# Graph message passing on one core: the edge stage on pairs of chunks, with a new order of GpSimd's work

## The chip, the cores and the metric

The kernel runs on one core of a Trainium2 chip. The metric is the device time of one execution in microseconds (us), the median over runs. The engines are TensorE (PE, its weight loads PEld), VectorE (DVE), ScalarE (ACT), GpSimd (POOL) and SyncE (SP, which only issues transfers). Each works through its own instructions in order and waits on semaphores.

## The reference

There are 50000 nodes with 256 numbers each and 12500 edges, sorted by destination. Two layers are computed; the change concerns the edges of the first.

```python
h = relu(layernorm(x))                      # every node
xn = layernorm(h) * ln_g + ln_b
q, k, v = xn @ Wq.T + bq, xn @ Wk.T + bk, xn @ Wv.T + bv
dk = silu(edge_attr @ Wdk.T + bdk);  dv = silu(edge_attr @ Wdv.T + bdv)
attn = silu(sum(q[dst] * k[src] * dk, 1)) * cosine_cutoff(edge_weight)
agg = segment_sum(v[src] * dv * attn[:, None], dst)
x = x + h + agg @ Wo.T + bo                 # end of layer 1
# layer 2: deg by src, dinv = rsqrt(deg), normalised gather over the edges (rows dst into src),
# then h @ (W, W1), relu, @ W2, added to x
```

## The kernel before, in words

The edges are cut into 98 chunks of 128 edges, one edge a partition; the nodes into 98 groups of 512 rows. Five stages follow each other: a set-up (weights transposed, degrees summed with one-hot matmuls, their inverse roots written to a table in DRAM), the edge stage of layer 1 (`messages`), the edge stage of layer 2 (`messages2`, 49 pairs of chunks), the node stage (`nodes`, 98 groups), and the last stores. `sums0` and `sums1` in DRAM hold the sums; they are filled with their first values by 512 KB transfers from SP (`rows_b`, `rows_0`), and for part of `sums0` from ACT in the first steps of the edge stage.

Each engine has its own function `messages(s)`, called once a step by `run_steps`; in it blocks for different chunks stand in a fixed order, `s.back(n)` being the chunk n steps back. For one chunk the edge stage does this:

- POOL gathers 128 rows of x for the destinations and 128 for the sources by indirect transfers (`gather_x`, four chunks ahead of use, into X2, a ring of four), and one number an edge from the table (`tab_d`).
- DVE takes the statistics of the two tiles (`bn_stats`, `bn_aggr`, L751 and L773) and adds eps (`ve`); POOL raises them to the power -0.5 (`inv_sqrt`, L476); DVE makes the bias `nb`. ACT computes the normalised relu into H2 (`m_h`). DVE takes the statistics of H2, in the same instructions as those of a later chunk; the same power call serves both; ACT scales H2 into Z2 (`m_z`).
- PE transposes Z2 and the edge attributes (bank 0 and 7), ACT copies bank 0 to `zT`, DVE copies the attributes to `aT`. PE makes the 512 numbers dk, dv (bank 1; ACT takes the silu into `DS`), k and v (banks 2 and 3), q (bank 4), each with a bias from a matmul on three rows (`ones3`, `bias3`).
- DVE: k * dk (`KD`), the sum with q (`at`), ACT its silu (`sa`), DVE times the cutoff (`aa`) and the message `MSG`. DVE also compares the destinations within the chunk (`EQ`) and finds which edge is the first of its node (`cnt`, `fst`, `sidx`); the others are sent to dump rows.
- PE sums equal destinations (MSG with EQ, bank 5), DVE copies it (`ST`), PE multiplies with Wo (bank 6), ACT copies it (`UB`), POOL adds its rows to `sums0` by an indirect transfer (`scatter_add`, L480).
- DVE keeps x + h of the destinations (`kept`) and ew * dinv (`norm`) for `messages2`.

POOL's order in a step before is: the two row gathers of chunk s, the power for chunk s-1, the table gather of s-1, the scatter of chunk s-11. Every scatter waits for the one before to have landed (`m_sc`).

Of the kernel before, what the change touches and what calls it, by code (L numbers as in the profile page):

```python
# [5 lines left out]
P = 128  # L6
D = 256
R = 64
N = 50000
# [4 lines left out]
G = 4  # L14
# [6 lines left out]
MESSAGE_STEPS = 11  # L21
# [5 lines left out]
FILLS_STEP = 4  # L27
# [62 lines left out]
def build(nc, x, src, dst, edge_attr, edge_weight, ln_g, ln_b, Wq, bq, Wk, bk, Wv, bv, Wo, bo,  # L90
          Wdk, bdk, Wdv, bdv, W, b, W1, b1, W2, b2, out):
    ctx = ExitStack()
    with ctx:
# [13 lines left out]
        sums0 = nc.dram_tensor("sums0_dram", (ROWS, D), F32).ap()  # L107
# [12 lines left out]
        ones3 = sb("ones3", [3, P], BF16)  # L120
        leave3 = sb("leave3", [3, 2])
# [9 lines left out]
        def place(taken, shape, dt=F32):  # L131
# [4 lines left out]
            at0 = taken[0]  # L136
# [11 lines left out]
        def temp(shape, dt=F32):  # L148
# [18 lines left out]
        rows3 = temp([3, 4 * D])  # L167
        part3 = temp([3, 4 * D])
        piece = temp([3, 4 * D], BF16)
        bias3 = sb("bias3", [3, 4 * D], BF16)  # L170
# [25 lines left out]
        dump_f = sb("dump_f", [P, 1])  # L196
        dump_i = sb("dump_i", [P, 1], I32)
# [32 lines left out]
        X2 = [CG[1][:, i, :].rearrange("p (a d) -> p a d", a=2) for i in range(4)]  # L230
        H2 = [CG[2][:, i, :].rearrange("p (a d) -> p a d", a=2) for i in range(4)]
        Z2 = ring("z2_", 2, [P, 2, D])
        ib = ring("ib_", 2, [P, 2, 3], I32)
        attr = ring("attr_", 4, [P, R])
        row_d = ring("row_d_", 4, [P, P], I32)

        st = ring("st_", 2, [P, 4, 6])
        mv = ring("mv_", 2, [P, 4, 2])
        ve = ring("ve_", 2, [P, 4, 1])
        rs = ring("rs_", 2, [P, 4, 1])  # L240
        nb = ring("nb_", 2, [P, 4, 1])
        zT = ring("zT_", 2, [P, 2 * KC, P])
        aT = ring("aT_", 2, [R + 1, P])
        DS = ring("ds_", 2, [P, 2 * D])
        KD = ring("kd_", 2, [P, D])
        junk = sb("junk", [P, D])
        junk_e = sb("junk_e", [P, P])
        at = ring("at_", 2, [P, 1])
        sa = ring("sa_", 2, [P, 1])
        aa = ring("aa_", 2, [P, 1])  # L250
        EQ = ring("eq_", 2, [P, P])
        MSG = ring("msg_", 2, [P, D])
        ST = ring("stt_", 2, [P, KC, P])
        UB4 = sb("ub4", [P, 4, D])
        UB = [UB4[:, i, :] for i in range(4)]
        tab_d = ring("tab_d_", 2, [P, 2, 1])
        cnt = ring("cnt_", 2, [P, 2])
        fst = ring("fst_", 2, [P, 2])
        sidx = ring("sidx_", 2, [P, 2], I32)
        m_ib, m_row, m_attr = sem("m_ib"), sems("m_row", 4), sems("m_attr", 4)  # L260
        m_x, m_tab = sems("m_x", 4), sems("m_tab", 2)
        (m_st, m_mv, m_ve, m_rs, m_nb, m_h, m_z, m_xh, m_T, m_zT, m_aT, m_D, m_qkv, m_ds, m_kd, m_at, m_sa, m_aa,
         m_eq, m_cnt, m_fst, m_idx, m_msg, m_S, m_ST, m_U, m_UB, m_keep) = [
            sem("m_" + n) for n in ("st mv ve rs nb h z xh T zT aT D qkv ds kd at sa aa eq cnt fst idx msg S ST U "
                                    "UB keep").split()]
# [9 lines left out]
        EQ2 = [halved(CG[2], i)[:, 2:4, :] for i in range(2)]  # L275
        EN = ring("en_", 2, [P, 2, 2 * P])
# [61 lines left out]
        def _(sp):  # L338
# [21 lines left out]
            for i, v in enumerate((bq, bk, bv, b2)):  # L360
                sp.dma_start(rows3[:, i * D:(i + 1) * D],
                             v.rearrange("(a d) -> a d", a=1).broadcast_to([3, D])).then_inc(s_ldw, 16)
# [7 lines left out]
            for i in range(FILLS_FIRST):  # L370
                sp.dma_start(group(sums0, Step(i)), rows_b).then_inc(s_fill, 16)

# [4 lines left out]
            LATER = 8  # L377

            def load_edges(s):
                k = s  # L380
                if k.within(EC):
                    n = k.off if k.reg is None else None
                    rows = ET if n == EC - 1 else P
                    if k.past(4):

                        pass_on(sp, (m_T, k.value(-3)))
                    sp.dma_start(attr[k.slot(4)][0:rows, :],
                                 edge_attr[bass.ds(k.value(0, P), rows), :]).then_inc(m_attr[k.slot(4)], 16)
                    if k.past(4):

                        pass_on(sp, (m_eq, k.value(-3)))
                    sp.dma_start(row_d[k.slot(4)][:, 0:rows],
                                 dst[bass.ds(k.value(0, P), rows)].rearrange("(a e) -> a e", a=1)
                                 .broadcast_to([P, rows])).then_inc(m_row[k.slot(4)], 16)

                k = s.back(LATER)
                if k.within(EC):

                    sp.dma_start(group(sums1, k), rows_0).then_inc(s_fill1, 16)

            assert NG == EC
            run_steps(sp, EC, LATER, 4, 4, load_edges)
# [47 lines left out]
        def _(pool):  # L450
# [36 lines left out]
            def gather_x(k):  # L487

                for i in range(2):
                    gather(X2[k.slot(4)][:, i, :], x, ib[k.pair()][:, k.slot(2), i:i + 1], last_node, m_x[k.slot(4)])  # L490


            pool.wait_ge(m_ib, 2)
            for i in range(4):
                gather_x(Step(i))

            def messages(s):
                k = s
                if k.within(EC) and k.past(4):

                    w = [(m_xh, k.value(-3))]
                    if k.slot(2) == 0:
                        w.append((m_ib, k.turns(2, 1)))
# [836 lines left out]
```

## Time and profile before

| | us |
|---|---|
| median of 3 runs (lowest, highest) | 2039.34 (2038.46, 2040.52) |
| the profiled execution, its own time | 2035.36 |
| its span in the trace | 2033.7 |
| mean granted TensorE clock, share of full | 0.900 |
| busy: PE, DVE, ACT, POOL | 1667.5, 1406.6, 1193.9, 1389.7 |

The busy times are sums over all stages; what matters for the change is the stretch from about 107 us, where the DVE begins with chunk 0, to about 848 us, where the first gather of `messages2` starts. In rows of the timeline the first number is the start and the second the duration, in us from the start of the span.

### The profile page before, as it was taken

To read this page: it belongs to the slowest core of one execution; us is meant where nothing else is said; L and a number is where in the kernel's file an instruction comes from. 1 tells how busy PE (TensorE), PEld (TensorE's weight loads), DVE (VectorE), ACT (ScalarE), POOL (GpSimd) and SP (SyncE) were. 2 spreads that over 40 slices of the span, in tenths; PEclk is the share of its full clock that TensorE was granted. 3 is DMA by queue.
4 is the path that set the end of the run, shared out by engine and by line. 5 is a ranking of instruction groups with operands and counts; after the bars stand their busy time and mean duration, and the time that the engine had idled before them with its cause. 6 is when DMAs were issued, how large, how long until landed. Compare 5 with 4: busy or idle time off the path is not lost.

```text
span 2033.7 us, 32020 instructions
## 1 busy us (share of the span) xinstructions
PE 1667.5 (82%) x6331; PEld 1026.7 (50%) x6331; DVE 1406.6 (69%) x5976; ACT 1193.9 (59%) x2320; POOL 1389.7 (68%) x1047
## 2 busy tenths in 40 slices
PE   4939999999999999344444541999999999999999
PEld 2315454445544545233333331676767666666666
DVE  7956666666666666355545547888888888888883
ACT  5925555554555454122222124998898989898884
POOL 2047888888888885488888877666666666666660
PEclk9959999999999999666656655999999999999999
DMA  7996555555555556244445458899999999999991
GB/s 247 418 363 204 142 146 150 140 143 143 154 140 142 145 144 203 47 87 89 89 89 90 87 102 206 234 272 273 263 272 269 269 270 268 272 269 267 266 256 72
DMA packets 170410, 391.76 MB, mean 193 GB/s; under 512 B 38847, under 2 KB 85872, under 8 KB 170368
## 3 DMA queue, kind: packets, MB, share of 16 engines
q1 hardware_dynamic: 105920, 257.96, 37.6%
q0 software_dynamic: 59552, 115.52, 31.0%
q10 hardware_dynamic: 4896, 17.83, 2.2%
q8 instruction: 13, 0.21, 0.0%
q14 instruction: 29, 0.24, 0.0%
HBM read 211.37 MB, written 179.85 MB: 192 GB/s over the span
## 4 chain that ended last, share of the span: by engine, by line
POOL 31%; DMA 22%; PE 18%; issue 16%; DVE 9%; SPq 2%; ACT 1%; POOLq 1%; DVEq 0%; ACTq 0%
POOL sums_dram L480 8%; DMA sums_dram<-ub,sidx 8%; POOL cg L484 7%; DMA out_dram<-cg 6%; POOL kept L567 6%; PE bank L1312 6%; PE bank L1301 6%; POOL b_rs L476 4%; DMA cg<-in_x_dram,ib 4%; PE bank L1169 3%; DVE cg L929 3%; POOL tab_d L484 3%; DMA cg<-sums_dram,ic 3%; POOL rs L476 2%; PE bank L1291 1%
## 5 line engine op out<-in xcount | busy, mean ns | idle before, releaser
L480 POOL DMA_INDIRECT sums_dram<-ub,sidx x196 | 318.9, 1627 | 96.8 <-issue 42.7
L1301 PE MATMUL bank<-kept,w 128*128 128x512 f32 x784 | 354.6, 595 | 0.0
L1312 PE MATMUL bank<-w_sb,kept 128*128 128x256 f32 x1568 | 354.3, 379 | 0.0
L567 POOL TENSOR_TENSOR kept<-kept 128x1024 f32<-128x1024 f32 x98 | 233.4, 2382 | 176.4 <-DVE cg L929 176.4
L1267 PE MATMUL bank<-cg,en 128*128 128x256 f32 x392 | 178.3, 634 | 204.4 <-ACT cg L1074 197.6
L1312 PEld LDWEIGHTS bank<-w_sb,kept 128*128 128x128 f32 x1568 | 297.9, 190 | 81.9 <-issue 46.4
L484 POOL DMA_INDIRECT cg<-in_x_dram,ib x196 | 206.3, 1052 | 78.9 <-issue 58.4
L1267 PEld LDWEIGHTS bank<-cg,en 128*128 128x128 f32 x392 | 120.5, 322 | 262.1 <-issue 236.4
L476 POOL TENSOR_TENSOR b_rs<-b_ve,minus_half 128x8 f32<-128x8 f32 x102 | 209.8, 2057 | 23.7 <-DVE b_ve L946 23.7
L476 POOL TENSOR_TENSOR rs<-ve,minus_half 128x4 f32<-128x4 f32 (+1 forms) x149 | 145.2, 974 | 101.4 <-DVE ve L781 91.6
L1301 PEld LDWEIGHTS bank<-kept,w 128*128 128x128 f32 x784 | 142.2, 191 | 141.9 <-issue 141.8
L1095 ACT ACTIVATE kept<-kept,b_nb,b_rs 128x256 f32<-128x256 f32 x392 | 202.2, 589 | 13.4 <-DVE b_nb L919 13.4
L1105 ACT ACTIVATE kept<-kept,b_nb,b_rs 128x256 f32<-128x256 f32 x392 | 202.3, 589 | 9.6 <-DVE b_nb L919 9.6
L1224 PE MATMUL bank<-qkv_w,zT 128*128 128x512 f32 x392 | 198.0, 628 | 0.0
L1065 ACT ACTIVATE ub<-bank 128x512 f32<-128x512 f32 x49 | 29.2, 597 | 273.6 <-DMA sums_dram<-ub,sidx 273.6
L1014 ACT ACTIVATE ub<-bank 128x256 f32<-128x256 f32 x98 | 37.7, 384 | 258.0 <-PE bank L1251 243.0
L751 DVE BATCH_NORM_STATS2 st<-cg 128x6 f32<-128x256 f32 x196 | 73.7, 418 | 163.4 <-DMA cg<-in_x_dram,ib 158.8
L957 DVE SCALAR_TENSOR_TENSOR kept<-cg,dinv,kept 128x256 f32<-128x256 f32 x392 | 163.9, 480 | 5.0 <-issue 2.2
L1086 ACT ACTIVATE kept<-bank 128x1024 f32<-128x1024 f32 x98 | 100.4, 1024 | 85.7 <-PE bank L1291 85.7
L929 DVE TENSOR_TENSOR cg<-kept,bank 128x1024 f32<-128x1024 f32 x98 | 119.6, 1220 | 39.3 <-PE bank L1312 34.7
L1291 PE MATMUL bank<-identity,kept 128*128 128x128 f32 x784 | 103.9, 276 | 51.6 <-DVE kept L957 51.5
L934 DVE BATCH_NORM_STATS2 b_st<-kept 128x6 f32<-128x256 f32 x392 | 137.0, 412 | 3.2 <-DMA kept<-in_x_dram 3.2
(183 smaller groups left out, 3227.7 us busy)
## 6 DMA issues: line engine op xcount, KB each, us to landing
sums_dram<-cg SPq DMA_DIRECT2D x162, 512.0 KB
kept<-in_x_dram SPq DMA_DIRECT2D x97, 512.0 KB, 5.8
kept<-sums_dram POOLq DMA_DIRECT2D x97, 512.0 KB, 9.9
cg<-sums_dram SPq DMA_DIRECT2D x97, 512.0 KB, 8.8
out_dram<-cg SPq DMA_DIRECT2D x97, 512.0 KB, 9.7
sums_dram<-cg ACTq DMA_DIRECT2D x34, 512.0 KB
row_d<-in_dst_dram SPq DMA_DIRECT2D x97, 64.0 KB
row_s<-in_src_dram SPq DMA_DIRECT2D x48, 128.0 KB
```

Of the source, the lines that this page charges most:

```text
L476: pool.tensor_tensor(to, var, minus_half[:, 0:width].rearrange("p (a b) -> p a b", b=1), ALU.pow).then_inc(done, 1)
L480: pool.indirect_dma_start(sums, bass.IndirectOffsetOnAxis(idx, 0), rows, None, bounds_check=last_row, compute_op=ALU.add).then_inc(done, 16)
L484: pool.indirect_dma_start(to, None, table, bass.IndirectOffsetOnAxis(idx, 0), bounds_check=bound, oob_is_err=True).then_inc(done, 16)
L567: pool.tensor_tensor(X1[k.slot(8)], X[k.slot(4)], H[k.slot(2)], ALU.add).then_inc(g_xh, 1)
L929: dve.tensor_tensor(OUT[k.slot(2)], X1[k.slot(8)], bank[:, to:to + 2, :].rearrange("p a b -> p (a b)"), ALU.add).then_inc(g_fin, 1)
L957: ins = dve.scalar_tensor_tensor(AG[k.slot(2)][:, at0], S1[k.slot(4)][:, at0], dinv[:, bass.ds(k.value(0, G) + j, 1)], H1[k.slot(2)][:, at ...
L1095: ins = act.activation(H1[k.slot(2)][:, j * D:(j + 1) * D], X1[k.slot(8)][:, j * D:(j + 1) * D], ACT.Relu, bias=b_nb[k.back(-4).slot(2)][: ...
L1105: ins = act.activation(H[k.slot(2)][:, j * D:(j + 1) * D], X[k.slot(4)][:, j * D:(j + 1) * D], ACT.Relu, bias=b_nb[k.slot(2)][:, j, :], sc ...
L1224: pe.matmul(bank[:, 2 + q, :], zT[q][:, KC + c, :], qkv_w[:, c, D:3 * D], start=False, stop=(c == KC - 1))
L1267: ins = pe.matmul(bank[:, q, to * D:(to + 1) * D], EN[q][:, i, to * P:(to + 1) * P], H1e[q][:, i, :], start=(i == 0), stop=(i == 1))
L1301: ins = pe.matmul(bank[:, 2 + m, :], w01[:, c, m * P:(m + 1) * P], hT[k.slot(2)][:, c * GN:(c + 1) * GN], start=(c == 0), stop=(c == KC - 1))
L1312: ins = pe.matmul(to, rT[k.slot(2)][:, c * GN + j * P:c * GN + (j + 1) * P], w2_sb[:, c, :], start=False, stop=(c == KC - 1), skip_group_c ...
```

## The change

All engines' `messages(s)` now handle a pair of chunks in a step: 49 pairs (`EP`), with 7 steps of depth instead of 11.

- POOL is unrolled in full. In its step p it does: the two scatters of pair p-7; the power for pair p-2 (one call on 128x6: the roots for both normalisations, the second variance being worked out as var(h) + eps times the first); `gather_x(p)`, that is four row gathers, the destinations' straight into `kept`; the two table gathers of pair p-1.
- DVE's step s works for the pairs a = s-1 (first statistics), g = s-2 (second statistics), z = s-3 (bias `nbz`, `kept`) and m = s-4 (attention, message), interleaved in the order of the diff.
- ACT's relu now runs before the first root is known (it only subtracts the mean, into G2), and ACT copies `ST`.
- The bias is folded into the weights: element 0 of each tile Z2 is a constant 1, since the normalised row sums to zero; the six bias matmuls of a pair go. The edge attributes arrive transposed by the host, so that their transpose and the copy to `aT` go too.
- EQ of the second chunk in a pair spans 256 edges (both chunks), so that equal destinations within a pair are summed once, and the two scatters of a pair may be in flight together: PE has 6 matmuls of 128 columns a pair for that instead of 4.
- SP fills `sums1` by two transfers a pair; ACT fills the rest of `sums0` by 8 transfers a step (4 before). `norm` is one instruction after the stage. The temporaries of the set-up lie at the other end of `kept`.

```diff
-            def messages(s):
-                k = s
-                if k.within(EC) and k.past(4):
-                    w = [(m_xh, k.value(-3))]
...
-                    gather_x(k)
-                k = s.back(1)
-                if k.within(EC + 2):
-                    inv_sqrt(ve[k.slot(2)][:, :, :], rs[k.slot(2)][:, :, :], m_ve, m_rs, k)
-                if k.within(EC):
...
-                    gather(tab_d[k.pair()][:, k.slot(2), :], table, ...
-                k = s.back(11)
-                if k.within(EC):
...
-                    scatter_add(sums0, sidx[k.pair()][:, k.slot(2):k.slot(2) + 1], UB[k.slot(4)], m_sc)
+            def gather_x(p):
+                if p >= 2:
+                    pool.wait_ge(m_h, p - 1)
+                for k in (2 * p, 2 * p + 1):
+                    gather(XS[k % 4], x, look[:, k, 1:2], last_node, m_x[p % 2])
+                    gather(kept[:, k, :], x, look[:, k, 0:1], last_node, m_x[p % 2])
+            def messages(p):
+                k = p - 7
+                if 0 <= k < EP:
+                    pool.wait_ge(m_UB, k + 1)
+                    pool.wait_ge(m_idx, k + 1)
+                    if k >= 1:
+                        pool.wait_ge(m_sc, 32 * k)
...
+                    for i in range(2):
+                        scatter_add(sums0, sidx[:, 2 * k + i:2 * k + i + 1], UB[2 * (k % 2) + i], m_sc)
+                k = p - 2
+                if 0 <= k < EP:
...
+                    pool.wait_ge(m_ve, k + 1)
+                    pool.tensor_tensor(RS[k % 2]..., VE[k % 2][:, 1:4, :, :]..., minus_half..., ALU.pow).then_inc(m_rs, 1)
+                if p < EP:
+                    gather_x(p)
+                k = p - 1
+                if 0 <= k < EP:
...
+                    for i in (2 * k, 2 * k + 1):
+                        gather(tab_d[:, i, :], table, look[:, i, 2:3], last_entry, m_tab)
```

```diff
+            def messages(s):
...
+                a, g, z, m = s.back(1), s.back(2), s.back(3), s.back(4)
+                if a.within(EP):
+                    q = a.slot(2)
+                    dve.wait_ge(m_x[q], a.turns(2, 64))
+                    for i in range(2):
+                        dve.bn_stats(st1[q][:, 0, i, :], XS[2 * q + i])
...
+                if z.within(EP):
+                    q = z.slot(2)
+                    dve.wait_ge(m_rs, z.value(1))
...
+                    dve.scalar_tensor_tensor(nbz[q][:, :, :], mv2[q][:, :, :, 0], -1.0, RS[q][:, 1:3, :, 0],
+                                             ALU.mult, ALU.mult).then_inc(m_nb, 1)
...
+                if g.within(EP):
+                    q = g.slot(2)
+                    dve.wait_ge(m_mv2, g.value(1))
+                    dve.wait_ge(m_ve1, g.value(1))
+                    dve.scalar_tensor_tensor(VE[q][:, 2:4, :, 0], VE[q][:, 0:2, :, 0], EPS, mv2[q][:, :, :, 1],
+                                             ALU.mult, ALU.add).then_inc(m_ve, 1)
```

The order of a step s after the change, in full (each with the waits that the prediction speaks of):

- DVE: a: 4 `bn_stats` of the gathered rows (waits `m_x`, both chunks' four gathers). m: `key(0)` (KD; waits `m_kv`, `m_ds`). z: `nbz` (waits `m_rs`, gives `m_nb`). a: 4 `bn_aggr`. m: `attend(0)`. a: `nm1` (gives `m_nm1`), eps. z: 2 `kept` (gives `m_keep`). m: 2 `EQ`. g: 4 `bn_stats` (waits `m_h`). m: 2 `cnt`, `key(1)` (waits `m_kv` and `m_ds` of the second chunk). g: 4 `bn_aggr`. m: `attend(1)` (waits `m_q`, gives `m_at`), `fst`. g: the last part of `VE` (gives `m_ve`). m: `sidx`, `aa` (waits `m_sa`), 2 `MSG` (gives `m_msg`).
- ACT: the fills (steps 2 to 6); m: `zT` of the first chunk; s-7: `UB`; m: `DS` of the first chunk; z: 2 of `Z2`, first chunk (waits `m_nb`); m: `zT` of the second chunk; z: 2 of `Z2`, second chunk; pair s-1: 4 relu (waits `m_nm1`, and `m_keep` of pair s-3; gives `m_h`); m: `DS` of the second chunk (gives `m_ds`); s-5: `ST`; m: the silu of `at`.
- PE: m: dk/dv, k/v (waits `m_zT`, and `m_msg` of the pair before) and q of the first chunk, transposes of the second; s-5: MSG with EQ; m: dk/dv, k/v, q of the second chunk; s-6: Wo; s-3: transposes of the first chunk.

## Rows read from the trace of the kernel before

**Rows 1.** Stretches: busy PE, PEld, DVE, ACT, POOL, granted clock, DMA share, GB/s.

```profile
400.00:600.00 200.00, 185.90 (x719) 100.59 (x720) 134.58 (x666) 102.19 (x228) 167.58 (x144) 1.00 0.55 145
...
900.00:1100.00 200.00, 100.28 (x219) 67.43 (x217) 103.36 (x486) 42.46 (x81) 167.19 (x136) 0.62 0.50 89
```

**Rows 2.** Groups of GpSimd's instructions, 200 to 800 us: busy, mean; idle before, releaser.

```profile
L484 POOL DMA_INDIRECT cg<-in_x_dram,ib x166 | 175.0, 1054 | 50.8 <-issue 50.8
L480 POOL DMA_INDIRECT sums_dram<-ub,sidx x86 | 139.4, 1620 | 29.6 <-issue 25.6 <-ACT ub L1014 4.0
L476 POOL TENSOR_TENSOR rs<-ve,minus_half 128x4 f32<-128x4 f32 x86 | 94.2, 1095 | 4.7 <-DVE ve L781 2.1
L484 POOL DMA_INDIRECT tab_d<-table_dram,ib x84 | 90.5, 1077 | 16.0 <-issue 14.1 <-DVE sidx L813 1.0 <-DVE norm L817 0.4
```

**Rows 3.** Timeline of GpSimd in one step of the edge stage.

```profile
501.82 1.07 POOL L484 DMA_INDIRECT tab_d<-table_dram,ib  x1 [0.19 <-issue]
503.20 1.62 POOL L480 DMA_INDIRECT sums_dram<-ub,sidx  x1 [0.30 <-issue]
505.13 1.07 POOL L484 DMA_INDIRECT cg<-in_x_dram,ib  x1 [0.31 <-issue]
506.51 1.03 POOL L484 DMA_INDIRECT cg<-in_x_dram,ib  x1 [0.31 <-issue]
```

**Rows 4.** Groups by form, whole span: the power at two widths.

```profile
L476 POOL TENSOR_TENSOR b_rs<-b_ve,minus_half 128x8 f32<-128x8 f32 x102 | 209.8, 2057 | 23.7 <-DVE b_ve L946 23.7
...
L476 POOL TENSOR_TENSOR rs<-ve,minus_half 128x4 f32<-128x4 f32 x100 | 109.3, 1093 | 94.5 <-DVE ve L781 91.6
```

**Rows 5.** Timeline of VectorE, ScalarE and one PE group in the same step.

```profile
502.29 0.60 ACT L1021 ACTIVATE zT<-bank 128x512 f32<-128x512 f32 x1
...
502.79 1.08 ACT L1030 ACTIVATE z<-cg,nb,rs 128x256 f32<-128x256 f32 x2
...
503.36 1.98 PE L1224 MATMUL bank<-qkv_w,zT 128*128 128x512 f32 x4
503.77 1.08 ACT L1039 ACTIVATE cg<-cg,nb,rs 128x256 f32<-128x256 f32 x2
...
504.70 0.75 DVE L751 BATCH_NORM_STATS2 st<-cg 128x6 f32<-128x256 f32 x2 [2.52 <-DMA cg<-in_x_dram,ib]
...
505.37 0.41 DVE L755 CUSTOM_DVE_ANT_0 junk<-bank,kd 128x256 f32<-128x256 f32 x1
505.70 0.08 DVE L755 DVE_READ_ACCUMULATOR2_ANT at<- 128x1 f32 x1
...
505.93 0.58 ACT L1054 ACTIVATE ds<-bank 128x512 f32<-128x512 f32 x1
...
506.60 0.38 DVE L773 BATCH_NORM_AGGREGATE mv<-st 128x2 f32<-128x6 f32 x4
...
508.76 0.16 DVE L741 SCALAR_TENSOR_TENSOR nb<-mv,rs 128x4 f32<-128x4 f32 x1
...
508.83 0.42 DVE L747 TENSOR_TENSOR kd<-bank,ds 128x256 f32<-128x256 f32 x1
```

**Rows 6.** Timeline of PE in the first steps of the stage.

```profile
137.24 1.12 PE L1205 MATMUL bank<-identity,z 128*128 128x128 f32 x4 [5.75 <-ACT z L1030]
...
140.74 3.78 PE L1224 MATMUL bank<-qkv_w,zT 128*128 128x512 f32 x4
```

**Rows 7.** The chain of waits in order of time: start, duration of the piece.

```profile
351.92 3.75 DMA cg<-in_x_dram,ib
...
499.54 5.14 DMA cg<-in_x_dram,ib
...
982.54 2.88 DMA cg<-sums_dram,ic
```

**Rows 8.** Timeline of GpSimd at both ends of the stage.

```profile
117.83 1.09 POOL L484 DMA_INDIRECT tab_d<-table_dram,ib  x1 [8.30 <-DMA table_dram<-dinv]
...
848.17 1.10 POOL L484 DMA_INDIRECT cg<-sums_dram,ic  x1 [2.51 <-DMA sums_dram<-ub,sidx]
```

More of the change, by code:

```diff
@@ L26 @@
 FILLS_FIRST = 64
[L27 removed]
+FILLS_STEP = 8
 CUTOFF = 5.0
@@ L257, in build @@
         cnt = ring("cnt_", 2, [P, 2])
         fst = ring("fst_", 2, [P, 2])
[L259 to L265, printed above, removed]
+        sidx = sb("sidx", [P, EC], I32)
@@ L530, in _ @@
+            pool.wait_ge(m_ib, 1)
+            for p in range(EP + MESSAGE_STEPS):
+                messages(p)
             pool.wait_ge(m_sc, 16 * EC)
@@ new lines, in messages, with scaled @@
+                if s.back(4).within(EP):
+                    silu_d(0)
+                def scaled(i):
+                    k = s.back(3)
+                    q = k.slot(2)
+                    act.wait_ge(m_nb, k.value(1))
+                    if k.past(1):
+                        act.wait_ge(m_T, k.value(-1, 2) + i + 1)
+                    for e in range(2):
+                        ins = act.activation(Z2[i][:, e, 1:D], G2[2 * q + i][:, e, 1:D], ACT.Identity,
+                                             bias=nbz[q][:, e, i:i + 1], scale=RS[q][:, 1 + e, i, :])
+                    ins.then_inc(m_z, 1)
@@ L1033, in messages @@
-                k = s.back(2)
-                if k.within(EC):
-                    act.wait_ge(m_nb, k.value(1))
-                    if k.past(4):
-                        act.wait_ge(m_xh, k.value(-3))
-                    for i in range(2):
-                        ins = act.activation(H2[k.slot(4)][:, i, :], X2[k.slot(4)][:, i, :], ACT.Relu,
-                                             bias=nb[k.slot(2)][:, i, :], scale=rs[k.slot(2)][:, i, :])
-                    ins.then_inc(m_h, 1)
-                k = s.back(7)
@@ L1180, in _ @@
                                     start=(k == 0), stop=(k == KC - 1))
+            for i, w in enumerate((0, 512)):
+                wide = min(512, 3 * D - w)
+                ins = pe.matmul(bank[:, i, 0:wide], first_row[:, :], qkv_w[:, 0, w:w + wide], start=True, stop=True)
             ins.then_inc(s_pre_pe, 1)
@@ new lines, in messages @@
+                if m.within(EP):
+                    project(0)
+                    turn(m, 1)
+                if f.within(EP):
+                    q = f.slot(2)
+                    pe.wait_ge(m_msg, f.value(1, 2))
+                    pe.wait_ge(m_eq, f.value(1))
+                    if f.past(1):
+                        pe.wait_ge(m_ST, f.value(0))
+                    for c in range(KC):
+                        own, rest = MSG[0][:, c * P:(c + 1) * P], MSG[1][:, c * P:(c + 1) * P]
+                        pe.matmul(bank[:, 5, c * P:(c + 1) * P], own, EQ[0][q][:, :], start=True, stop=False)
+                        pe.matmul(bank[:, 5, c * P:(c + 1) * P], rest, EQ[1][q][:, 0:P], start=False, stop=True)
+                        ins = pe.matmul(bank[:, 5, (KC + c) * P:(KC + c + 1) * P], rest, EQ[1][q][:, P:2 * P],
+                                        start=True, stop=True)
+                    ins.then_inc(m_S, 1)
@@ L1234, in messages @@
-                k = s.back(8)
-                if k.within(EC):
-                    pe.wait_ge(m_msg, k.value(1))
-                    pe.wait_ge(m_eq, k.value(1))
-                    if k.past(1):
-                        pe.wait_ge(m_ST, k.value(0))
-                    for c in range(KC):
-                        ins = pe.matmul(bank[:, 5, c * P:(c + 1) * P], MSG[k.slot(2)][:, c * P:(c + 1) * P],
-                                        EQ[k.slot(2)][:, :], start=True, stop=True)
-                    ins.then_inc(m_S, 1)
```

535 lines of the change are left out of this document (287 added, 248 removed).

## The prediction

> **What bounds the kernel now.** I read the stretches first, for where the edge stage lies and which engine is fullest. In it PE is busy 185.9 of 200 us at full clock, and POOL 167.6 [rows 1]. The groups of GpSimd's instructions then show why POOL looks less full than it is. From 200 to 800 us it did 86 chunks, 6.98 us each. Its busy time is 175.0 + 139.4 + 94.2 + 90.5 = 499.1 us, and nearly all of its idle time is "issue" (50.8 + 25.6 + 14.1 = 90.5 us), only some 10 us are waits for somebody [rows 2]. The timeline shows this issue time in place: 0.30 to 0.31 us ahead of each indirect transfer, 0.19 us behind the power [rows 3]. So POOL sets the pace before, with PE close behind, and each chunk costs what POOL's five instructions cost. The latencies (a gather takes 3.8 to 5.1 us from its start to landing [rows 7]) are mostly covered, because the gathers run four chunks ahead of use.
>
> The question for the change is therefore double: what POOL's work of a pair costs, and whether the new order still keeps the latencies off the path.
>
> **POOL's own work for a pair.** Four row gathers, 1.05 us each, and two table gathers, 1.08 [rows 2]; two scatters, 1.62; 0.31 us of issue ahead of each [rows 3]. The power on 6 numbers is not in the trace: 4 cost 1.09 and 8 cost 2.06 [rows 4], so between these; I take 1.57, about the middle. Sum: two scatters 3.86, power 1.57, first row gather 0.19 + 1.05, three more 4.08, two table gathers 2.78: 13.5 us a pair, against 13.96 before. What the unrolling saves in registers I cost at nothing, as the 0.31 us belongs to the transfers. If POOL still set the pace, the change would bring 0.5 us a pair.
>
> **The loop that the new order closes.** In its step p POOL waits for `m_ve` of pair p-2, does the power, and only then gathers the rows of pair p. `m_ve` of pair p-2 comes near the end of DVE's step p (g = s-2). DVE's step p+1 begins with the wait for exactly the rows of pair p (a = s-1). Nothing runs ahead: behind the waiting power stand the gathers on POOL's queue; behind the waiting `bn_stats` stands all of DVE's step on DVE's, the end of which releases the next power. The period C of a step is at least the way round:
>
> 1. *From the rows' landing to* `nb`: four `bn_stats`, two take 0.67 us from start to the next one's start, so 1.33; `key(0)` in between, 0.33 to the next start; `nbz` 0.16: 1.8 us [rows 5].
> 2. *ACT from* `m_nb` *to the second* `DS`: two of `Z2`, `zT`, two of `Z2`, four relu, then `DS`. Two 256-wide activations take 0.98 us from start to the next start (502.79 to 503.77), `zT` 0.50, `DS` 0.58 to its end: 4 x 0.98 + 0.50 + 0.58 = 5.0 us [rows 5], and 0.05 for the signal. DVE's own work meanwhile (statistics of g, `kept`, EQ, counts: some 4 us) is hidden under this; without ACT's queue it would bind at about 7.0 us instead of the 8.2 below.
> 3. *DVE from* `m_ds` *to* `m_ve`: `key(1)` 0.42, four `bn_aggr` 0.3, `attend(1)` 0.41 + 0.08 [rows 5], two small ones 0.2: 1.4 us. So landing to `m_ve` is D = 8.2 us if PE's k/v and q of the second chunk are there in time. They start when the second `zT` is done (1.8 + 0.98 + 0.60 = 3.4 us) and end at 3.5 + 1.98 + half of that = 6.5, in time at full clock.
> 4. *POOL from* `m_ve` *to the start of the last gather*: signal 0.05, power 1.57, issue 0.19, three gathers at 1.36: 5.9 us.
> 5. *The landing* L of the last gather from its start: 3.75 and 5.14 us in the edge stage, 2.88 in `messages2`, where no 512 KB fills run beside it [rows 7]. The fills of a pair are released by EQ, some 4 us into DVE's step, and 1 MB of them should be through before the gathers start, so I take 3.2, and 2.8 to 5.1 as bounds.
>
> With full clock throughout: 8.2 + 5.9 + 3.2 = 17.3 us, against 13.96 before.
>
> **PE's clock.** PE is busy 6.5 us a chunk before [rows 1]; without the bias matmuls and with one more matmul of MSG a chunk about 5.9, so 11.8 of 17.3 us. Its idle time comes in one piece: k/v of the second chunk waits for `zT`, which stands behind the scaling, which waits for `nb`: 5 to 7 us idle, ahead of just the matmuls that step 3 needs. After 5.75 us of idleness PE ran the same transposes and k/v projection at half speed (3.78 us instead of 1.98, the level of 1.2 GHz instead of 2.4) [rows 5, 6], and in `messages2`, with shorter pauses, the granted clock averages 0.62 [rows 1]. From half speed the second q is there at 3.5 + 3.78 + 1.7 = 9.0 us, and `m_ve` at 9.0 + 0.5 + 0.2 = 9.7 to 9.8. That is D's upper end; I take 9.4, since PE, two thirds busy, will not be slow each time. C = 9.4 + 5.9 + 3.2 = 18.5 us.
>
> The Trainium skill (TensorE: Matmul & The Clock Gate, "HAM oscillation") warns against this shape, bursts of matmuls parted by a wait for data, and has each burst start at the low clock. By it D would be 9.8 and the time some 18 us longer; the rows of the first steps agree with it.
>
> Of the landing, the Trainium skill (DMA: Bandwidth & Descriptors, "Anatomy of one DMA") gives about 2.0 us fixed and the bytes over 436 GB/s, so an estimate of 2.3 us for these 128 KB; the rows are all above, perhaps as theirs is from the start of GpSimd's instruction. With 2.3 us C would be 17.6 and the time 40 us shorter.
>
> **The whole stage.** Before, the first gather of `messages2` starts at 848.2 us [rows 8]. After: the power of step 2 comes after the first table gathers, which wait for the table, at 117.8 + 2 x 1.39 = 120.6 us [rows 8]. Steps 3 and 4 lack the attention part but have 8 fills a step in ACT's queue; my estimate is 16 us each, so `m_ve` of step 4 at 152. Steps 5 to 49 gather rows: 45 x C. Steps 50 to 52 have no rows to wait for and run at PE's pace, 11.5 us each; then S, ST, Wo and UB, about 3.5, and the last two scatters 1.93 + 1.55 + 2.51 to their landing [rows 8]: 44 us. End: 152 + 45 C + 44 = 196 + 45 C, which is 1028.5 for C = 18.5, 180 us later than before. Break-even is C = 14.5.
>
> The rest is nothing or small. The set-up loses the three-row bias work and gains `weights()` (six DVE instructions), both hidden under the wait for the table, until 117.8. DVE loses `ST`, `aT`, half of the small instructions, and gains wider EQ; ACT gains `ST`: in the loop these count only as in the sum above. The waits of the scatters (for UB, for the scatters of the pair before) come 5 us and more ahead of the power and are met a step earlier; the scatters and table gathers (6.6 us) run while DVE works, under C - 5.9 - 1.4. If the loop went away, they would be POOL's bound of 13.5. SP's fills have 18 us a pair instead of 14 and are ready earlier. The stages behind are the same code: no change.
>
> Sum: the profiled execution took 2035.4 us, 4 below the median. 2035.4 + 180 = 2215, and as a median 2219 us.
>
> **The rivals.**
>
> *Short loop.* PE stays warm and the rows land as in `messages2`: C = 8.2 + 5.9 + 2.8 = 16.9, end at 956.5, 2148 us as a median. For it: fewer fills beside the gathers, PE two thirds busy. Against it: the idle piece lies just ahead of the projection that counts.
>
> *Long loop.* The projections always start slow and the fills hold the gathers up: 9.8 + 5.9 + 5.1 = 20.8, 2323 us. PE's whole pair at half speed, 11.8 x 1.9 = 22, would be the pace itself; but PE busy without pause came back to full clock (3.78 us at 140.7, 1.98 at 503.4 [rows 5, 6]), so it shouldn't last.
>
> *POOL remains the bound, faster.* C = 13.5: end at 803.5, 1995 us. This needs D + L below 13.5 - 5.9 = 7.6 us, or rows that are gathered a step earlier than I read. Against it: ACT's and DVE's sum of 8.2 alone is above that, and so is DVE's own 7.0 with any landing of the rows. If half the loop were hidden by something I don't see, C would be near 14.5 and the time unchanged.
>
> **How the numbers follow.** Forecast (C 17.5 to 19.5, 2175 to 2264 us) 0.55; short loop 0.19; long loop 0.17; POOL the bound 0.06; near 14.5 0.03, of which 0.02 within 0.2% (about what a measurement of this kernel tells from no change, 4 us) and 0.01 above. Predicted is the likeliest, 2219. The range goes a little past the short loop and halfway into the long one: 2130 to 2300. Faster 0.06, same 0.02, slower 0.92.
>
> **What would show it.** In the changed kernel's edge stage: a period of 18.5 us a pair, POOL waiting for DVE's last part of VE at each power, some 4 to 5 us; DVE's first `bn_stats` of a step waiting for the gathers, some 8 us; PE idle in one piece of 5 us or more ahead of the second k/v, with a granted clock under 1; the first `messages2` gather near 1030 us, and 1185 us from there to the end as before. The prediction is wrong if POOL shows issue time alone between its instructions (then the gathers run ahead after all), if the power waits but DVE's wait for rows is short (then D is mis-sized), or if the stages behind change.

## The result and the profile after

The changed kernel takes 2186.25 us (median of 4 runs, 2185.38 to 2187.83), the kernel before 2038.9 us beside it (2038.21 to 2040.52): a ratio of 1.0722, interval 1.0704 to 1.0741. The change makes the kernel 147 us slower. Forecast were 2219 us and a range of 2130 to 2300. The profiled execution took 2185.38 us, with a span of 2183.7 us.

First the stretches of the changed kernel (start and end, length, busy us with the number of instructions for PE, PE's weight loads, DVE, ACT and POOL, granted clock, DMA share, GB/s):

```profile
200.00:400.00 200.00, 147.89 (x564) 91.63 (x562) 94.27 (x448) 80.05 (x172) 129.26 (x108) 0.91 0.43 115
400.00:600.00 200.00, 152.53 (x556) 94.25 (x557) 94.39 (x452) 82.37 (x178) 125.30 (x103) 0.88 0.45 120
```

Where 200 us of the edge stage had 185.9 us of PE and 167.6 of POOL before [rows 1], there are now 152.5 and 125.3: every engine is less full than it was. None of them can be the bound. Then GpSimd's groups from 200 to 950 us (busy us, mean ns of one | idle us ahead of them and what ended it), to set beside [rows 2]:

```profile
L483 POOL DMA_INDIRECT sums_dram<-ub,sidx x88 | 147.6, 1678 | 26.9 <-issue 26.9
L487 POOL DMA_INDIRECT cg<-in_x_dram,look x86 | 91.8, 1067 | 22.1 <-issue 22.1
L487 POOL DMA_INDIRECT tab_d<-table_dram,look x88 | 89.0, 1011 | 26.7 <-issue 26.7
L487 POOL DMA_INDIRECT kept<-in_x_dram,look x86 | 88.3, 1027 | 26.2 <-issue 26.2
L516 POOL TENSOR_TENSOR rs<-ve,minus_half 128x6 f32<-128x6 f32 x45 | 61.1, 1359 | 178.7 <-DVE ve L829 175.6 <-DVE sidx L834 3.1
```

The transfers cost what they did. New is the last row: ahead of 45 powers POOL stands idle for 178.7 us, and 175.6 of them end with DVE's VE. The waits of all engines over the same stretch show the other members of the same ring (engine, tile, line <- releaser: sum us, count, longest):

```profile
ACT z L1068 <- DVE nbz L761: 315.6, 44, 7.5
DVE st L735 <- DMA kept<-in_x_dram,look: 314.5, 43, 7.6
...
PE bank L1280 <- ACT zT L1038: 186.3, 43, 4.5
POOL rs L516 <- DVE ve L829: 175.6, 44, 8.3
```

Each is met some 43 times in 43 pairs: DVE waits for rows that POOL gathered, ACT for DVE, PE for ACT, POOL for DVE. One trip round in the middle of the stage, from the timeline (start, us, engine, line, tile, idle before it and who ended that):

```profile
507.67 1.36 POOL L516 TENSOR_TENSOR rs<-ve,minus_half 128x6 f32<-128x6 f32 x1 [3.75 <-DVE ve L829]
509.23 1.12 POOL L487 DMA_INDIRECT cg<-in_x_dram,look  x1 [0.19 <-issue]
...
513.32 1.01 POOL L487 DMA_INDIRECT kept<-in_x_dram,look  x1 [0.30 <-issue]
...
516.13 0.75 DVE L735 BATCH_NORM_STATS2 st<-cg 128x6 f32<-128x256 f32 x2 [7.17 <-DMA kept<-in_x_dram,look]
...
517.97 1.09 ACT L1068 ACTIVATE z<-cg,nbz,rs 128x255 f32<-128x255 f32 x2 [7.31 <-DVE nbz L761]
...
519.59 3.46 PE L1280 MATMUL bank<-qkv_w,zT 128*128 128x512 f32 x4 [4.37 <-ACT zT L1038]
...
522.24 0.57 ACT L1056 ACTIVATE ds<-bank 128x512 f32<-128x512 f32 x1
...
523.09 0.42 DVE L745 TENSOR_TENSOR kd<-bank,ds 128x256 f32<-128x256 f32 x1 [1.30 <-PE bank L1280]
...
524.38 0.15 DVE L829 SCALAR_TENSOR_TENSOR ve<-ve,mv 128x4 f32<-128x4 f32 x1
...
524.71 1.36 POOL L516 TENSOR_TENSOR rs<-ve,minus_half 128x6 f32<-128x6 f32 x1 [3.79 <-DVE ve L829]
```

Read it as a circle. From power to power 17.04 us: 5.65 to the start of the last gather (513.32 - 507.67), 2.81 to DVE's `bn_stats` on its rows (516.13), 8.40 to the end of VE (524.53) and 0.18 to the next power. It is tight everywhere: 1.84 us from the rows to ACT's first scaling, 4.84 from there to the end of the second `DS` (522.81), 0.28 more until PE's slow k/v is done (519.59 + 3.46 = 523.05), and 1.44 from `key(1)` to the end of VE.

The stage as a whole, by the first table gather, the power of step 3 and the first gather of `messages2` in POOL's timeline:

```profile
123.30 1.01 POOL L487 DMA_INDIRECT tab_d<-table_dram,look  x1 [94.42 <-DMA table_dram<-dinv]
...
142.66 1.36 POOL L516 TENSOR_TENSOR rs<-ve,minus_half 128x6 f32<-128x6 f32 x1 [7.73 <-DVE ve L829]
...
991.09 1.09 POOL L487 DMA_INDIRECT cg<-sums_dram,ic  x1 [2.53 <-DMA sums_dram<-ub,sidx]
```

The table's gather starts at 123.3 instead of 117.83, and the first gather of `messages2` at 991.09 instead of 848.17 [rows 8]: of the 150 us between the two profiled executions 142.9 lie before it and 7 behind. The power of step 3, at 142.66, still waited 7.73 us, twice what it does later.

### The profile page after: what moved, and what is told of

It is laid out like the page before. It is cut to its first block, busy times and chain, and to the rows that moved or that the text cites. A ratio compares the mean times of both kernels' runs of the same rounds, so it can differ in the third digit from the quotient of the medians.

```text
span 2183.7 us, 30280 instructions
## 1 busy us (share of the span) xinstructions
PE 1652.2 (76%) x6241; PEld 1070.0 (49%) x6241; DVE 1344.8 (62%) x5623; ACT 1184.3 (54%) x2271; POOL 1345.6 (62%) x996
## 4 chain that ended last, share of the span: by engine, by line
PE 26%; POOL 25%; DMA 21%; issue 11%; DVE 10%; ACT 4%; SPq 1%; DVEq 1%; POOLq 1%; ACTq 0%
PE bank L1280 8%; DMA out_dram<-cg 7%; DMA kept<-in_x_dram,look 7%; POOL cg L487 6%; PE bank L1381 6%; PE bank L1370 6%; POOL kept L569 5%; DMA sums_dram<-ub,sidx 4%; POOL b_rs L479 3%; DMA cg<-sums_dram,ic 3%; POOL sums_dram L483 3%; PE bank L1221 3%; POOL rs L516 3%; DVE cg L952 3%; POOL kept L487 2%
## 5 line engine op out<-in xcount | busy, mean ns | idle before, releaser
L1280 PE MATMUL bank<-qkv_w,zT 128*128 128x512 f32 x392 | 263.5, 810 | 210.5 <-ACT zT L1038 210.5
L483 POOL DMA_INDIRECT sums_dram<-ub,sidx x196 | 324.0, 1653 | 83.9 <-issue 42.4
L1068 ACT ACTIVATE z<-cg,nbz,rs 128x255 f32<-128x255 f32 x196 | 106.1, 590 | 352.1 <-DVE nbz L761 352.1
L1280 PEld LDWEIGHTS bank<-qkv_w,zT 128*128 128x128 f32 x392 | 88.6, 249 | 357.7 <-ACT zT L1038 268.9
L735 DVE BATCH_NORM_STATS2 st<-cg 128x6 f32<-128x256 f32 x98 | 36.9, 418 | 365.5 <-DMA kept<-in_x_dram,look 365.5
L516 POOL TENSOR_TENSOR rs<-ve,minus_half 128x6 f32<-128x6 f32 x49 | 66.6, 1359 | 207.6 <-DVE ve L829 204.6
L487 POOL DMA_INDIRECT tab_d<-table_dram,look x98 | 99.1, 1011 | 123.9 <-DMA table_dram<-dinv 94.4
```

What stands on the lines that cost most here:

```text
L483: pool.indirect_dma_start(sums, bass.IndirectOffsetOnAxis(idx, 0), rows, None, bounds_check=last_row, compute_op=ALU.add).then_inc(done, 16)
L487: pool.indirect_dma_start(to, None, table, bass.IndirectOffsetOnAxis(idx, 0), bounds_check=bound, oob_is_err=True).then_inc(done, 16)
L1280: ins = pe.matmul(bank[:, 2 + i, :], zT[i][:, c, :], qkv_w[:, c, D:3 * D], start=(c == 0), stop=(c == KC - 1))
```

## The experiments

Every kernel below is the changed kernel with the edit shown, and every ratio is to the kernel before, timed beside it; "period" is the time from power to power in the edge stage.

**Rows gathered ahead of the power.** If the loop is closed by POOL's order alone, moving one call must undo the slowdown.

```diff
+                if p < EP:
+                    gather_x(p)
                 k = p - 2
...
-                if p < EP:
-                    gather_x(p)
```

> The changed kernel with one block of GpSimd moved: in a step the four row gathers stand ahead of the power. Loop theory: the wait for m_ve no longer holds the gathers up, so the loop is cut and GpSimd's own work sets the pace: two scatters 3.95, four row gathers 5.4, power 1.36, two table gathers 2.5, together 13.2 us a pair instead of 17.1; 46 steps x 3.9 = 180 us less than the changed kernel's 2186: 2006 us. Rival 1 (the pairs themselves are slow: k/v banks with one buffer a chunk, PE and ScalarE in a chain over the message): no change, 2170 to 2190. Rival 2 (GpSimd's busy time sets the pace): no change either, since its work is the same.

Measured: 2002.46 us, ratio to before 0.9834 (0.9817 to 0.9851), 184 us under the changed kernel and 34 under the one before (2036.67 us beside it). The period is 13.2 us. POOL's timeline of one step:

```profile
504.14 1.09 POOL L487 DMA_INDIRECT cg<-in_x_dram,look  x1 [0.30 <-ACT cg L1088]
...
508.24 1.01 POOL L487 DMA_INDIRECT kept<-in_x_dram,look  x1 [0.30 <-issue]
509.28 1.36 POOL L518 TENSOR_TENSOR rs<-ve,minus_half 128x6 f32<-128x6 f32 x1
510.83 1.07 POOL L487 DMA_INDIRECT tab_d<-table_dram,look  x1 [0.19 <-issue]
512.21 1.03 POOL L487 DMA_INDIRECT tab_d<-table_dram,look  x1 [0.30 <-issue]
513.54 1.62 POOL L483 DMA_INDIRECT sums_dram<-ub,sidx  x1 [0.30 <-issue]
515.47 1.57 POOL L483 DMA_INDIRECT sums_dram<-ub,sidx  x1 [0.31 <-issue]
517.35 1.09 POOL L487 DMA_INDIRECT cg<-in_x_dram,look  x1 [0.30 <-ACT cg L1088]
```

Nothing but issue time stands between the instructions: the power starts right behind the last gather, and this is the picture of [rows 3] again, with POOL as the bound. 13.21 us from 504.14 to 517.35 is POOL's own work for a pair, measured. The waits say the same:

```profile
POOL rs L518 <- DVE ve L829: 4.3, 2, 2.3
```

Two waits of 4.3 us in all from 200 to 780 us, where the changed kernel has 137.8 in the same stretch. So the whole loss is the place of `gather_x`; all the rest of the change together gains 34 us. POOL's work for a pair is 13.21 us instead of 13.96, and one power on 6 numbers in place of two on 4 saves 0.82 of it (1.36 for 2 x 1.09), about all.

**Rows gathered one pair further ahead, behind the power.** This keeps the wait in front of the gathers, but gives the rows a step more to land.

```diff
+            gather_x(0)        # ahead of the loop
...
-                if p < EP:
-                    gather_x(p)
+                if p + 1 < EP:
+                    gather_x(p + 1)
```

> The changed kernel with GpSimd's order kept (scatters, power, rows, tables), but the rows gathered behind the power are those of pair p+1 instead of p. Loop theory: what costs is the distance, not the order, so this too should give about 13.2 us a pair and 2006 us. Only if the gathers' wait for the relu (m_h) now comes late would it be more, 14 to 15 us a pair, 2040 to 2090. Rival 1 and rival 2: no change, 2170 to 2190.

Measured: 2026.79 us, ratio 0.9948 (0.993 to 0.9965). The period is 13.95 us on the mean, going to and fro between 13.0 and 14.9.

```profile
POOL rs L516 <- DVE ve L830: 23.0, 23, 1.6
```

160 us come back, but not all 184, and the time lies between the two that were expected (2006, or 2040 to 2090): some power in two still waits for DVE, up to 1.6 us. POOL no longer waits for what it gathered itself, and is just short of being the bound. Why 0.75 us a pair is left isn't settled (last experiment).

**No table gathers.** The rival: POOL is slow because of its work, and 98 transfers fewer must shorten the step.

```diff
-                    for i in (2 * k, 2 * k + 1):
-                        gather(tab_d[:, i, :], table, look[:, i, 2:3], last_entry, m_tab)
...
-            link(dve.tensor_tensor(norm[:, :], tab_d[:, :, 0], ew_f[:, :], ALU.mult))
+            link(dve.tensor_copy(norm[:, :], ew_f[:, :]))
```

> The changed kernel without the 98 table gathers; the norm of the second layer's edges is then edge_weight alone. Loop theory: they run behind the row gathers while VectorE works and GpSimd waits 3.8 us for VE2 afterwards, so the period stays at 17.1 and the time at 2186 within 8 us. Rival 2 (GpSimd's busy time sets the pace): 2.65 us a pair less, 2186 - 125 = 2061.

Measured: 2180.54 us, ratio 1.0708 (1.069 to 1.0726), period 17.04 to 17.08. 2.6 us of POOL's work a step, gone, bring 5.7 us in the whole kernel, and in the profiled executions 3.8 us of that are there at the first power (121.90 for 125.66 us), before any step of the loop. The kernel leaves the table's factor out of the second layer. POOL waits longer instead, up to 7.2 us a time (here from 200 to 780 us, with 34 steps):

```profile
POOL rs L516 <- DVE ve L825: 225.6, 34, 7.2
```

**The same cut with the rows gathered first.** The counter-test, an edit to the kernel of the first experiment, with the table's factor left out as before: where POOL is the bound, the same 98 transfers must cost their time.

```diff
-                    for i in (2 * k, 2 * k + 1):
-                        gather(tab_d[:, i, :], table, look[:, i, 2:3], last_entry, m_tab)
```

> The version with the row gathers ahead of the power, and without the table gathers (the second layer's norm is then edge_weight alone). If in that version GpSimd's own work is the bound, the same removal that gave 6 us in the changed kernel now gives up to 2.6 us a pair, down to PE's 11.8: 1.4 us x 46 = 64 at least, 2002 - 64 = 1938 (1900 to 1945). Rival (that version is bound by PE and the chain over the message at 13.2): no change, 1996 to 2002.

Measured: 1924.82 us, ratio 0.9443 (0.9422 to 0.9463): 77.6 us less than with the table gathers, where the other order gave 5.7. The period falls from 13.2 to 11.7 us on the mean over the stage (11.4 in its middle); the full 2.6 us do not come, as POOL then begins to wait for ACT (21.6 us from 200 to 650 us, for `UB`) and DVE (7.6 us).

**The power twice.** What stands between the wait and the last gather must cost its full time each step.

```diff
                 if 0 <= k < EP:
                     ...
+                    pool.tensor_tensor(RS2[...], VE[k % 2][...], minus_half[...], ALU.pow)
                     pool.tensor_tensor(RS[...], VE[k % 2][...], minus_half[...], ALU.pow)
```

> The changed kernel with the power done twice in each step, the first time into a scratch tile. Loop theory: the power lies in the loop, so each of 48 steps is 1.36 to 1.4 us longer: 2186 + 66 = 2252. Rival 1 (PE and ScalarE chain over the message sets the pace): GpSimd has 3.8 us of slack, so no change, 2186.

Measured: 2275.45 us, ratio 1.1167 (1.1145 to 1.1189). That is 89 us more, where 1.35 us over 48 steps are 65. The steps are longer by more than what was put in: 19.01 us on the mean over 48 steps, against 17.15, so 1.86 more. The timeline shows where the rest comes from:

```profile
502.26 0.75 DVE L739 BATCH_NORM_STATS2 st<-cg 128x6 f32<-128x256 f32 x2 [8.70 <-DMA kept<-in_x_dram,look]
...
505.72 3.78 PE L1284 MATMUL bank<-qkv_w,zT 128*128 128x512 f32 x4 [5.59 <-ACT zT L1042]
...
509.29 1.91 PE L1291 MATMUL bank<-qkv_w,zT 128*128 128x256 f32 x4
...
512.00 1.36 POOL L517 TENSOR_TENSOR rs<-ve,minus_half 128x6 f32<-128x6 f32 x1 [4.95 <-DVE ve L833]
513.35 1.32 POOL L520 TENSOR_TENSOR rs<-ve,minus_half 128x6 f32<-128x6 f32 x1
```

PE idles 5.6 us instead of 4.4, and the k/v projection behind it takes 3.78 us, all of it at half speed. The q projection is slow as well, 1.91 us instead of 1.03, and it is q that DVE's `attend(1)` then waits for. From `bn_stats` to the next power it is 9.74 us in this step (512.00 - 502.26), 9.3 on the mean of 41 steps, instead of 8.6 in the changed kernel (8.40 + 0.18). Not every step is like it: in 25 of the 41 it is 9.5 us or more, in 8 it is 8.9 to 9.0, and in 8 it is 8.5 to 8.6 as in the changed kernel. The granted clock fell with it:

```profile
200.00:780.00 580.00, 413.07 (x1457) 254.70 (x1458) 248.92 (x1194) 214.06 (x460) 369.00 (x301) 0.81 0.39 107
```

A delay put into the loop makes PE's pause longer, and with the longer pause PE is slower in the loop in most steps. That the pause is the cause is tested below, by filling it.

**ACT's second zT ahead of the scaling**, and **with the second DS behind it.** These shorten ACT's stretch of the loop without a change to anybody's work.

```diff
-                if s.back(3).within(EP):
-                    scaled(0)
                 if s.back(4).within(EP):
                     turned(1)
+                if s.back(3).within(EP):
+                    scaled(0)
```

The second kernel has this as well:

```diff
                     turned(1)
+                    silu_d(1)
...
-                if s.back(4).within(EP):
-                    silu_d(1)
```

> The changed kernel with ScalarE's copy zT of the second chunk moved ahead of the scaling that waits for m_nb, so that PE's second k/v projection no longer waits for the power. Loop theory: the loop loses zT (0.5 us on ScalarE) and no longer holds the slow k/v; rows to m_ve falls from 8.6 to about 7.85 us, the period from 17.1 to 16.4: 2186 - 33 = 2153, and the granted clock may be anything without moving it. Rival (VectorE's own work of 8.6 us is what fills the stretch, ScalarE's order is hidden): no change, 2186.

> As the one before, and ScalarE's second silu DS moved to the same place, ahead of scaling and relu. Loop theory: now nothing of ScalarE or PE stands between VectorE's nbz and key(1); VectorE's own work is left, about 7.2 us from rows to m_ve, period 15.8: 2186 - 61 = 2125. Still far over GpSimd's 13.2. Rival as before: no change, 2186.

Measured: 2138.53 us (2135.0 to 2140.74) with `zT` early, ratio 1.0492 (1.0466 to 1.0518), and 2106.51 us (2105.99 to 2108.15) with both, ratio 1.0335 (1.0313 to 1.0358). From `bn_stats` to the next power it is 7.6 and then 6.92 us (8.6 in the changed kernel), the period 16.05 and then 15.4. One step of the second kernel:

```profile
513.33 0.75 DVE L735 BATCH_NORM_STATS2 st<-cg 128x6 f32<-128x256 f32 x2 [7.19 <-DMA kept<-in_x_dram,look]
...
518.90 0.42 DVE L745 TENSOR_TENSOR kd<-bank,ds 128x256 f32<-128x256 f32 x1
...
520.25 1.36 POOL L516 TENSOR_TENSOR rs<-ve,minus_half 128x6 f32<-128x6 f32 x1 [2.13 <-DVE ve L829]
```

DVE's `key(1)` has no idle time ahead of it any more: between the rows and VE DVE now does only its own work, 6.74 us of it without the 0.18 of the signal. Thus DVE's own stretch stands right behind ACT's, near the 7 us of the prediction. 80 us are won, where 61 were expected (and 48 for 33 with `zT` alone): VE comes 0.25 us earlier in each step than the expectations had it, and the period is that much shorter and a little more. The loop still takes 15.4 us a pair, above POOL's 13.2.

**Matmuls into PE's pause.** Is PE's half speed on the path? This kernel gives PE 9 useless matmuls (each 256 columns wide, their output overwritten) ahead of the second k/v and nothing else to do.

```diff
                 def project(i):
                     ...
-                    pe.wait_ge(m_zT, k.value(0, 2) + i + 1)
                     if k.past(1):
                         pe.wait_ge(m_msg, k.value(-1, 2) + i + 1)
+                    for _ in range(9 * i):
+                        pe.matmul(bank[:, 3, 0:D], identity[:, :], w2_sb[:, 0, :], start=True, stop=True)
+                    pe.wait_ge(m_zT, k.value(0, 2) + i + 1)
```

> The changed kernel with nine extra 256-column matmuls of PE in its idle time ahead of the second k/v (into bank 3, which the projection overwrites). Loop theory with the clock as a term: PE has no pause, the clock stays at full, the second k/v takes 2.0 us instead of 3.5 and ScalarE's second DS is last: rows to m_ve 8.3 instead of 8.6, 2186 - 14 = 2172. Rival (the slow k/v comes from something else, such as its operands): k/v stays at 3.5 us and the time at 2186; if the fillers are in the way it is more.

Measured: 2176.8 us, ratio 1.068 (1.0655 to 1.0706): more work, and 9 us less than the changed kernel. The gain is small (the two ratios' intervals just touch), so the traces have to carry the argument. One step and the stretch:

```profile
511.21 4.05 PE L1279 MATMUL bank<-w_sb,identity 128*128 128x256 f32 x18
...
516.63 1.98 PE L1282 MATMUL bank<-qkv_w,zT 128*128 128x512 f32 x4 [1.38 <-ACT zT L1038]
...
519.97 0.42 DVE L745 TENSOR_TENSOR kd<-bank,ds 128x256 f32<-128x256 f32 x1 [1.13 <-ACT ds L1056]
...
521.32 1.36 POOL L516 TENSOR_TENSOR rs<-ve,minus_half 128x6 f32<-128x6 f32 x1 [3.35 <-DVE ve L829]
```

```profile
200.00:780.00 580.00, 531.15 (x2309) 374.91 (x2310) 280.05 (x1356) 243.87 (x524) 379.50 (x314) 1.00 0.45 122
```

The pause is 1.4 us, the clock 1.00, and the k/v projection takes 1.98 us: full speed. `key(1)` now waits for ACT's `DS`, no longer for PE, so from the rows to the next power it is the 8.05 to 8.15 us that ACT's queue sets, and the period is 16.55 us. The last power comes 15.7 us earlier than in the changed kernel (932.98 against 948.67 us), although two of the first steps, with the fills, take 22.1 and 24.9 us instead of 19.5 and 20.1; the last steps, which have the extra matmuls too, lose 7.7 us of it again.

**The power twice, with matmuls in the pause** (14 of them). If the excess of the doubled power was PE's clock, it must go.

> The power done twice as before, and 14 extra matmuls of PE in the longer pause ahead of the second k/v. With the power twice alone the period rose by 1.36 us (the power) and rows to m_ve from 8.57 to 9.2, which I put down to the clock. If so the fillers bring it back to 8.1 us: period 18.0 instead of 19.2, 2275 - 1.05 x 46 = 2227. Rival (the further 0.6 us came from something else in the longer step): 2270 to 2275.

Measured: 2244.11 us, ratio 1.1026 (1.1007 to 1.1044), 31 us less than without the matmuls. In the middle of the stage the period is 17.87 us: the 16.5 of the kernel with matmuls and 1.35 for the second power, with nothing added. The stretch is at full clock:

```profile
200.00:780.00 580.00, 560.00 (x2459) 407.70 (x2458) 262.12 (x1270) 226.96 (x487) 393.48 (x322) 1.00 0.41 112
```

The 17 us above the expectation lie outside this stretch: the first steps are part of it, two of which take 23.1 and 25.3 us.

**The two good orders together**: rows gathered ahead of the power (or one pair further ahead), and ACT's `zT` and `DS` early. The edits are those above.

> The row gathers ahead of the power and ScalarE's zT and DS of the second chunk ahead of scaling and relu, both. The ScalarE order brought 80 us where it lay in the loop. With the loop cut and GpSimd at 13.2 us a pair without waits it should bring nothing in the middle of the stage, at most 5 us at its ends: 1997 to 2003. Rival (the PE and ScalarE chain still holds that version): 1980 or less.

> GpSimd's order kept, rows gathered one pair further ahead (2027 us by itself, 13.95 us a pair instead of 13.2, with GpSimd waiting up to 1.6 us for VE2 in half its steps), and ScalarE's zT and DS of the second chunk moved ahead of scaling and relu. If what was left there is a second loop (power, nbz, scaling, zT, k/v, VE2), taking zT and DS out of it leaves GpSimd's own work: 13.2 us, 2027 - 35 = 1992 to 2000. Rival (the gathers' own wait for the relu or for landing makes the 0.75 us): no change, 2020 to 2027.

Measured, with the rows ahead of the power: 2000.26 us (1999.4 to 2001.3), ratio 0.9827 (0.9811 to 0.9843), with a period of 13.18. This is the fastest version that leaves nothing out, but the 2 us to the kernel with the rows first alone are within their intervals. With POOL as the bound, a shorter way through ACT is worth nothing.

Measured, with the rows one pair ahead: 2070.95 us, ratio 1.0177 (1.0144 to 1.021). This expectation failed: 44 us slower than the same kernel with ACT's old order. Its waits from 200 to 780 us and two lines of its timeline:

```profile
ACT zT L1039 <- PE bank L1261: 128.7, 33, 5.7
...
ACT ds L1057 <- remote: 102.3, 25, 5.1
...
DVE aa L838 <- ACT sa L1106: 69.0, 27, 3.0
```

```profile
513.04 0.60 ACT L1039 ACTIVATE zT<-bank 128x512 f32<-128x512 f32 x1 [5.38 <-PE bank L1261]
...
523.48 3.78 PE L1280 MATMUL bank<-qkv_w,zT 128*128 128x512 f32 x4 [2.49 <-ACT zT L1039]
```

ACT now reaches its `zT` before PE has written what it reads, and stands there for 128.7 us (4.1 with ACT's old order), with the scaling, relu, `ST` and the other silu queued behind. Ahead of `DS` it stands another 102.3 us (56.6 before), for which the profile names no engine; in the program `DS` waits for PE's dk/dv and for the message of the pair before. DVE waits for one of those (69.0 us), the message comes late, PE pauses 2.5 us and runs its k/v at half speed again. The edit that won 80 us where ACT was waiting for DVE at that point costs 44 where it wasn't.

## Why the prediction was right

**The loop** is the mechanism that was named, and it is shown: it opens when the gathers go first (-184 us), it hardly cares for POOL's work outside it (-5.7 us for 98 transfers fewer, and -77.6 for the same where there is no loop), and it follows what is put in or taken out of it. POOL waits 3.8 us a power (4 to 5 forecast), DVE 7.2 for rows (8), PE 4.4 in one piece (less than the 5 or more).

**The terms.** C was taken as 18.5 us and is 17.24 on the mean of the 45 steps, below even the 17.5 to 19.5 that the forecast allowed. That the time still fell inside its 2175 to 2264 us is in part luck: with 17.24 the same sum gives 2163, and the start, the end and the rest of the kernel were longer than summed. The terms by what they measured:

- *Rows to* `nb` 1.84 for 1.8, *ACT to the second* `DS` 4.84 for 5.0, *DVE to* `m_ve` 1.44 for 1.4: right.
- *D* is 8.4 us in most steps and 8.49 on the mean, for 9.4: the largest error, and it lies in PE's clock. Its ends hold. Without the signal of 0.18 it is 7.9 to 8.0 us at full clock with matmuls in the pause (8.2 forecast), 9.56 at its slowest with the power doubled (9.8), and 6.74 for DVE alone (7.0). But D was put too near the slow end. PE's k/v was slow each time, as said, yet in most steps the q projection behind it ran in 1.03 us, at full speed. So `key(1)` was 0.28 us late and `attend(1)` 0.15, and PE cost the loop 0.4 us where 1.2 were added for it. In five of the 45 steps q was slow in part (1.17 to 1.58 us), and in two from end to end:

```profile
536.87 3.78 PE L1280 MATMUL bank<-qkv_w,zT 128*128 128x512 f32 x4 [4.47 <-ACT zT L1038]
540.45 1.91 PE L1287 MATMUL bank<-qkv_w,zT 128*128 128x256 f32 x4
```

  There VE ended 9.56 us after the rows, and 9.42 in the step behind it, and these two periods are 18.44 and 18.06 us: the step that was forecast, but seldom. Why these two is open, as PE's pauses ahead of them, 4.47 and 3.95 us, are not longer than the others. The Trainium skill (TensorE: Matmul & The Clock Gate, "HAM oscillation") has every burst behind such a wait begin at the low clock. The trace agrees for the first matmuls, k/v with 3.46 us, and the whole burst slow, as the 9.8 took it, came in two of 45 steps alone.
- *POOL to the last gather* 5.83 for 5.9 from the end of VE: the power on 6 takes 1.36 us, not 1.57, and the signal 0.18, not 0.05. With the two means this makes 8.49 + 5.83 + 2.92 = 17.24.
- *Landing* 2.81 (2.92 on the mean of the 45 steps) for 3.2: as in `messages2` [rows 7]. The 5 us and more appear only in the first three steps, 5.8 to 6.5 us, beside the fills of the start. The estimate of 2.3 us from the Trainium skill (DMA: Bandwidth & Descriptors, "Anatomy of one DMA") is under all of them when counted from the start of GpSimd's instruction.

**The stage.** 45 steps took 775.6 us for 832.5 (-57). The power of step 4 came at 162.2 for 152 (+10), because the table's gather started 5.5 us later and steps 3 and 4 took 17.0 and 19.5 us for 16 each. The end of the stage, from the last of the 45 powers to the first gather of `messages2`, took 53.3 us for 44 (+9), and the rest of the kernel 1192.6 for 1185.5 (+7). Together -31 us; 2215.4 were forecast for the profiled execution and 2185.4 measured.

The end was too short because the sum counted the scatters of the last pair alone. Each pair's scatters wait for the landing of those of the pair before, and at the end three pairs' scatters follow each other 6.4 us apart (972.35, 978.70 and 985.15 us, then the gather at 991.09):

```profile
985.15 1.55 POOL L483 DMA_INDIRECT sums_dram<-ub,sidx  x1 [3.04 <-DMA sums_dram<-ub,sidx]
```

Of the 7 us in the rest, which were put at nothing because the code is the same, 6 lie in the node stage: POOL's 98 sums into `kept` there span 763.1 us instead of 757.4, and 762.5 in the kernel with the gathers first. What makes them is open.

The table is late because its own transfer takes 17.2 us instead of 12.1; that ACT's 8 fills of 512 KB beside it are the cause is only argued.

**POOL's own work** is 13.21 us a pair for 13.5, most of the difference being the power's.

**The rivals.** The short loop (16.9, 2148 us) was the nearest to the measurement after the forecast in time, and nearer than it in the period. The truth lies between the two: its landing and most of its clock, with a longer start and end. The long loop and POOL as the bound are false for this kernel; the latter is true, to 0.3 us, for the kernel with the gathers first.

**Open:** why the rows gathered one pair further ahead leave 13.95 us a pair instead of 13.2. That a second ring through the message, PE and ACT takes over is only argued from the last experiment, where lengthening ACT's waits made it worse; no run parts it from others.

## What to carry to other kernels

When an order of instructions is written out by hand, draw the ring that it closes: what the waiting instruction waits for, what is queued behind it, and whether that leads back to it. Here four gathers on the wrong side of one wait cost 184 us, where all the rest of the change gained 34. Test for such a ring by adding a known delay and by taking work off the engine outside it: in a ring the first costs its full time or more, and the second saves next to nothing. And moving a wait forward in an in-order queue pays only while its data are surely there: the same move gave 80 us in one order and cost 44 in the other.

## What the runs showed of the hardware

- Nine useless matmuls a pair (18 records, 4.05 us) made the kernel 9 us faster, and 14 of them 31 us with the power doubled: a pause of 4.4 us ahead of the k/v projection cost 1.5 us of it (3.46 instead of 1.98), one of 1.4 us nothing.
- The clock came back within the burst in most steps: k/v at 3.46 us, then q at 1.03, its time at full clock (as in the kernel with granted clock 1.00). In two steps of 45 q was slow from end to end as well (1.91 and 1.78 us), and with the power doubled in 25 of 41 (1.7 to 1.9 us).
- The power on 6 numbers a partition takes 1.36 us, on 4 1.09, on 8 2.06 [rows 4]: the time doesn't rise evenly.
- A delay of 1.35 us in the loop, the second power, lengthened the step by 1.86 us; with the clock held at 1.00 by matmuls it lengthened it by 1.3 (17.87 against 16.55).
